# Four-head attention sum: running states stored slot by slot, and one gather at the end in place of a masked copy at every column

## The reference

```
score[e, h] = leaky_relu(a_src[src[e], h] + a_dst[dst[e], h], 0.2)
top[n, h]   = max over the edges into n, and the loop edge, of score
w[e, h]     = exp(score[e, h] - top[dst[e], h])
sum[n, h]   = sum over the edges into n of w[e, h] * x[src[e]]      (64 wide)
out[n]      = mean over h of (sum[n, h] / total weight[n, h]) @ W[h] + bias
```

## Time and profile before

| | us |
|---|---|
| median of 3 runs | 10054.14 (10051.63 to 10055.38) |
| the profiled execution, its own time | 10059.48 |
| its span, from the first to the last instruction | 10057.3 |
| DVE busy over the span | 6330.4 (63%) |
| POOL busy over the span | 6560.1 (65%) |
| PE, ACT busy | 3022.2 (30%), 2917.7 (29%) |
| copies into `head` in the four-head stage, L1328 | 175.1 in 392 |
| head sums of the four-head stage, L1325 | 341.3 in 1568 |

### The profile page before, as it was taken

The page is one execution under the profiler, slowest core; times in us unless marked ns, Lnnn a source line. Parts: engine busy times, 40 slices in busy tenths (PEclk is TensorE's granted clock), DMA queues, the critical chain, the costliest instruction groups (busy, mean ns, idle before and its releaser), DMA issues. The chain is left out here.

```text
span 10057.3 us, 92986 instructions
## 1 busy us (share of the span) xinstructions
PE 3022.2 (30%) x15231; PEld 2811.3 (28%) x15231; DVE 6330.4 (63%) x18443; ACT 2917.7 (29%) x8172; POOL 6560.1 (65%) x6186
## 2 busy tenths in 40 slices
PE   3233002111114666500666634444400002333300
PEld 2132001111114555400655534444400002333300
DVE  8999887666664767500665579999644435666600
ACT  5366234333333444300433312222200002223200
POOL 2334017777776777577777757777677777666577
PEclk7566555555556878755555555555555555665555
DMA  1010271111113544411544511111111113434311
GB/s 53 14 30 24 98 234 26 25 25 25 25 22 101 158 148 155 134 43 50 182 170 169 177 43 48 47 47 47 39 44 45 44 42 105 112 108 115 91 45 40
DMA packets 455154, 791.99 MB, mean 79 GB/s; under 512 B 119922, under 2 KB 149611, under 8 KB 454559
## 3 DMA queue, kind: packets, MB, share of 16 engines
q1 hardware_dynamic: 252126, 560.13, 16.7%
q0 software_dynamic: 188448, 201.53, 9.2%
q10 hardware_dynamic: 14112, 26.10, 0.7%
HBM read 388.06 MB, written 425.04 MB: 81 GB/s over the span
## 5 line engine op out<-in xcount | busy, mean ns | idle before, releaser
L1056 POOL DMA_INDIRECT e_other<-X,e_from_rows x392 | 610.9, 1558 | 279.5 <-DVE e_fin L1343 143.2
L1720 POOL DMA_INDIRECT e_mine<-T,e_from_rows x392 | 400.7, 1022 | 569.3 <-DVE e_from_rows L1767 450.8
L743 POOL COPY sort_spare<-sort_words 128x768 f32<-128x768 f32 x272 | 369.2, 1379 | 606.9 <-DVE sort_words L802 396.9
L3395 POOL DMA_INDIRECT e4s_mine<-XA,e4s_from_rows x392 | 407.9, 1041 | 231.9 <-DVE e4s_from_rows L3449 124.3
L2209 PE MATMUL e_turned<-ident,e_own_x 128*128 128x128 f32 x196 | 54.6, 434 | 1573.6 <-ACT e_own_x L2121 1573.6
L2357 POOL DMA_INDIRECT e_mine<-X,e_from_rows x392 | 406.6, 1037 | 183.1 <-issue 112.5
L3416 POOL DMA_INDIRECT out_rows<-e4s_out,e4s_to_rows x392 | 385.2, 983 | 191.0 <-issue 191.0
L2378 POOL DMA_INDIRECT G<-e_g_slot,e_to_rows x392 | 385.2, 983 | 180.6 <-issue 119.0
L2865 POOL DMA_INDIRECT X<-e_row,e_to_rows x392 | 424.8, 1084 | 119.5 <-issue 116.1
L1070 POOL DMA_INDIRECT X<-e_row,e_to_rows x392 | 401.8, 1025 | 140.9 <-issue 118.2
L3398 POOL DMA_INDIRECT e4s_other<-X,e4s_from_rows x392 | 402.2, 1026 | 129.4 <-issue 127.6
(11 more groups left out here) (693 smaller groups left out, 15698.4 us busy)
## 6 DMA issues: line engine op xcount, KB each, us to landing
XA<-e_n_xa SPq DMA_DIRECT2D x49, 1056.0 KB
e4s_n_xa<-XA SPq DMA_DIRECT2D x49, 1056.0 KB, 6.3
X<-e_n_row SPq DMA_DIRECT2D x49, 576.0 KB
T<-pl_row SPq DMA_DIRECT2D x98, 272.0 KB
X<-e_n_row SPq DMA_DIRECT2D x49, 528.0 KB, 3.0
X<-pl_x ACTq DMA_DIRECT2D x98, 260.0 KB, 2.7
e_n_x<-X SPq DMA_DIRECT2D x49, 520.0 KB
G<-e_n_g SPq DMA_DIRECT2D x49, 512.0 KB, 2.8
```

Of the source, the lines that this page charges most:

```text
L1056: gp.indirect_dma_start(out=other[:, h, j, :], out_offset=None, in_=others[:, :], in_offset=bass.IndirectOffsetOnAxis(ap=from_rows[:, h, 1 ...
L1720: gp.indirect_dma_start(out=mine[:, h, j, :], out_offset=None, in_=g.T0[:, :], in_offset=bass.IndirectOffsetOnAxis(ap=from_rows[:, h, 0, j ...
L3395: gp.indirect_dma_start(out=mine[:, h, j, :], out_offset=None, in_=g.XA[:, :], in_offset=bass.IndirectOffsetOnAxis(ap=from_rows[:, h, 0, j ...
```

## The change

In the stage of four heads, DVE makes no more masked copies. SP stores the states of each chunk (128 partitions x 8 x 264 floats, 1056 KB) into a new DRAM table SUMS, one row per edge slot. Behind the last chunk, POOL gathers one row of 264 floats per partition into `head`. The row's number, `head_at`, is worked out once in `lay_out_edges`: 392*p - 1 plus the number of columns that belong to the partition's first run. The stage with one head keeps its copies.

With the copies the wait between columns goes too. It is replaced by a wait for the same head's sum of the column before, ahead of each of the sums but the first four of a chunk.

```diff
         dve = [Engine(sem(f"lay_dve{s}"), "diag flags count c0 c1 c2 c3 link ready") for s in range(ORDERS)]
...
+                gp.iota(at[:, :], pattern=[[1, 1]], base=-1, channel_multiplier=T).then_inc(const, 1)
...
+                    dve[s].done(v.tensor_reduce(fix[s][:, 5:6], g.first[s][:, :], AX.X, ALU.add), "count")
...
+                    v.tensor_tensor(g.head_at[s][:, :], fix[s][:, 5:6], at_f[:, :], ALU.add)
...
+                        if c[3]:
+                            n, h = c[3].n, c[3].slot
+                            sp.wait_ge(acc.sem, acc.after(n, summed))
+                            sp.nop(nofuse=True)
+                            sp.dma_start(slot_rows(g.SUMS, n), flat(state[:, h, :, :])).then_inc(sums_kept[h], 16)
...
                 stages(gp, NCH, RING, SKEW, body)
+                if kind == "heads":
+                    for h in range(RING):
+                        gp.wait_ge(sums_kept[h], len(range(h, NCH, RING)) * 16)
+                    gp.indirect_dma_start(out=head[:, :], out_offset=None, in_=g.SUMS[:, :],
+                                          in_offset=bass.IndirectOffsetOnAxis(ap=g.head_at[s][:, :], axis=0)).then_inc(head_back, 16)
...
                     if adding:
-                        row_numbers(adding)
+                        if kind == "edge":
+                            row_numbers(adding)
                         pay_out(adding)
...
+                    if kind == "heads":
+                        v.wait_ge(sums_kept[h], k * 16)
+                        if started:
+                            need(summed, n - 1)
...
-                        if j:
+                        if j and kind == "edge":
                             need(f"head{(j - 2) % J}")
                         for q in range(H):
                             part = slice(q * D, (q + 1) * D)
+                            if j and kind == "heads":
+                                need(f"run{j - 1}_{q}")
                             run = v.scalar_tensor_tensor(out=state[:, h, j, part], in0=before[:, part], scalar=ex[:, b, 0, j, q:q + 1],
                                                          in1=pay[:, j, part], op0=ALU.mult, op1=ALU.add)
-                        acc.done(run, f"run{j}")
-                        acc.done(v.copy_predicated(head[:, :], first[:, h if j else last, j - 1:j or J].to_broadcast([P, WSTATE]), before), f"head{(j - 1) % J}")
+                            acc.done(run, f"run{j}" if kind == "edge" else f"run{j}_{q}")
+                        if kind == "edge":
+                            acc.done(v.copy_predicated(head[:, :], first[:, h if j else last, j - 1:j or J].to_broadcast([P, WSTATE]), before), f"head{(j - 1) % J}")
...
                 end_state = state[:, LAST, J - 1, :]
-                v.wait_ge(acc.sem, acc.after(NCH - 1, f"head{J - 2}"))
-                v.copy_predicated(head[:, :], first[:, LAST, J - 1:].to_broadcast([P, WSTATE]), end_state).then_inc(set_up, 1)
-                v.wait_ge(set_up, 2)
+                if kind == "heads":
+                    v.wait_ge(acc.sem, acc.after(NCH - 1, summed))
+                    v.wait_ge(head_back, 16)
+                    v.sem_inc(set_up, 1)
```

More of the change, by code:

```diff
@@ L130, in lay_out_edges @@
         scat = [sb(f"lay_scat{s}", [P, T]) for s in range(ORDERS)]
-        ends = sb("lay_ends", [1, 2])
+        ends, at, at_f = sb("lay_ends", [1, 2]), sb("lay_at", [P, 1], I32), sb("lay_at_f", [P, 1])
         fix = [sb(f"lay_fix{s}", [P, 6]) for s in range(ORDERS)]
@@ L138, in lay_out_edges @@
         loaded, spread, turned = sem.pair("lay_loaded"), sem.pair("lay_spread"), sem.pair("lay_turned")
-        dve = [Engine(sem(f"lay_dve{s}"), "diag flags c0 c1 c2 c3 link ready") for s in range(ORDERS)]
+        dve = [Engine(sem(f"lay_dve{s}"), "diag flags count c0 c1 c2 c3 link ready") for s in range(ORDERS)]
         with nc.Block() as block:
@@ L937, in attend_edges @@
         to_rows = sb("to_rows", [P, RING, J], I32)
-        first = sb("first", [P, RING, J], I32)
+        first = sb("first", [P, RING, J], I32) if kind == "edge" else None
         mine = None if kind == "edge" else sb("mine", [P, RING, J, WOWN])
@@ L978, in attend_edges @@
             "heads": "sadd score keep top fall fallen rise"}[kind]), Engine(sem(f"{name}_act"), "ex")
-        acc = Engine(sem(f"{name}_acc"), "pay weight tops " + RUN_STEPS)
+        acc = Engine(sem(f"{name}_acc"), "pay weight tops " + (RUN_STEPS if kind == "edge" else " ".join(f"run{j}_{q}" for j in range(J) for q in range(H))))
         if kind == "heads":
@@ L996, in attend_edges @@
         LAST = (NCH - 1) % RING
+        summed = f"run{J - 1}" if kind == "edge" else f"run{J - 1}_{H - 1}"
         FIX = Chunk(0, NCH, RING)
@@ L1091, in _ @@
                 v.memset(top[:, RING - 1, :, :], NEG)
-                v.memset(head[:, :], 0.0)
-                v.memset(first[:, :, :], 0)
+                if kind == "edge":
+                    v.memset(head[:, :], 0.0)
+                    v.memset(first[:, :, :], 0)
                 v.memset(state[:, RING - 1, :, :], 0.0).then_inc(set_up, 1)
@@ L1148, in loop_logs @@
                         v.wait_ge(x3_loaded[h], (c.k + 1) * 16)
-                        v.wait_ge(acc.sem, acc.after(n, f"run{J - 1}"))
+                        v.wait_ge(acc.sem, acc.after(n, summed))
                         v.wait_ge(filed[h], c.k * 16 * J)
@@ L1306, in need @@
                         v.wait_ge(acc.sem, acc.after(m, step))
-                    v.wait_ge(flagged[h], k + 1)
-                    if kind == "edge" and begun(c, RING):
-                        v.wait_ge(sums_dve.sem, sums_dve.after(n - RING, "q0"))
-                    if started:
-                        need(f"head{J - 2}", n - 1)
+                    if kind == "heads":
+                        v.wait_ge(sums_kept[h], k * 16)
+                        if started:
+                            need(summed, n - 1)
+                    else:
+                        v.wait_ge(flagged[h], k + 1)
+                        if begun(c, RING):
+                            v.wait_ge(sums_dve.sem, sums_dve.after(n - RING, "q0"))
+                        if started:
+                            need(f"head{J - 2}", n - 1)
                     for q in range(H):
@@ L1389, in _ @@
                 end_state = state[:, LAST, J - 1, :]
-                v.wait_ge(acc.sem, acc.after(NCH - 1, f"head{J - 2}"))
-                v.copy_predicated(head[:, :], first[:, LAST, J - 1:].to_broadcast([P, WSTATE]), end_state).then_inc(set_up, 1)
-                v.wait_ge(set_up, 2)
+                if kind == "heads":
+                    v.wait_ge(acc.sem, acc.after(NCH - 1, summed))
+                    v.wait_ge(head_back, 16)
+                    v.sem_inc(set_up, 1)
+                else:
+                    v.wait_ge(acc.sem, acc.after(NCH - 1, f"head{J - 2}"))
+                    v.copy_predicated(head[:, :], first[:, LAST, J - 1:].to_broadcast([P, WSTATE]), end_state).then_inc(set_up, 1)
+                    v.wait_ge(set_up, 2)
                 for q in range(H):
@@ L3858, in gnn_kernel @@
     g.XH, g.G2S, g.B2S = dram("XH", EP, 2 * D), dram("G2S", EP, D), dram("B2S", EP, D)
-    g.X2S = dram("X2S", EP, D + 8)
+    g.X2S, g.SUMS = dram("X2S", EP, D + 8), dram("SUMS", EP, HEADS * D + 2 * HEADS)
     g.XA, g.X3S, g.OUTS = dram("XA", NP, 2 * D + 4), dram("X3S", EP, D + 2), dram("OUTS", EP, D)
@@ L3884, in gnn_kernel @@
         g.index = [sb(f"index{s}", [P, 3, T + 1], I32) for s in range(ORDERS)]
-        g.first = [sb(f"first{s}", [P, T], I32) for s in range(ORDERS)]
+        g.first, g.head_at = ([sb(f"{q}{s}", [P, width], I32) for s in range(ORDERS)] for q, width in (("first", T), ("head_at", 1)))
         g.pen, g.contrib, g.same = ([sb(f"{q}{s}", [P, T]) for s in range(ORDERS)] for q in ("pen", "contrib", "same"))
```

7 lines of the change are left out of this document (5 added, 2 removed).

## The result

| kernel | us, median (range, runs) | ratio to before, 95% interval |
|---|---|---|
| before | 10052.88 (10042.53 to 10055.38, 4) | |
| after | 9946.97 (9931.33 to 9952.29, 4) | 0.9894 [0.9877, 0.9911] |

The change takes 106 us off, 1.1%; the prediction said 113 and 9941. The two profiled executions are 10059.5 and 9952.3, 107 apart. How these 107 are made up is not how the prediction made them up, and the experiments are about that.

The account below looks back on a forecast made before the run. DVE bounds the four-head stage now, POOL next. Terms -31 (first iterations), -31 (slack), -75 (POOL's need), +22 (tail) and +2 (layout) sum to -113 us, from the median 10054.1 to 9941; range 9895 to 10005, chance 0.68.

Parts of the forecast that it names:

- POOL as the next bound: Four-head stage: DVE sets the pace at 27.8 us per iteration; once it is faster, POOL's need of 25.3 binds.
- Rival A: Four-head stage: DVE stays the bound, POOL's holds shrink or it has unseen room; -157 us, 9897; chance 0.13.
- DVE alone 23.9: Four-head stage: without the copies DVE alone would need 27.8 - 3.86 = 23.9 us per iteration.
- Slack until the bound: After the first iterations: POOL falls behind, its gathers' 9.0 us of slack lasting some 8 iterations at 3.86 gained; -31 us.
- 30 iterations at POOL's need: Remaining 30 iterations of the four-head stage: POOL binds at 25.3 us each in place of 27.8; -75 us.
- rival C: Four-head stage: POOL at its worst phase, need 26.8 us, with late landings; -41 us, 10013; chance 0.12.
- The waits at the sums: DVE's sums: the new waits and register instructions cost nothing; a chunk's 32 sums take about 6.3 us, 0.195 apart.
- Rival B: DVE's sums: the waits serialise them, 0.35 us each in place of 0.195; +86 us, 10140; chance 0.05.
- The stores at nothing: SP's queue: the 49 SUMS stores of 1056 KB cost zero, with 10 us kept for the range.
- The tail, +22: End of the four-head stage: the fix waits for the head gather behind all scatters, 127 us after iteration 48, not 105.4.
- Other stages within 3 us: Stages outside the change: the forecast is wrong if they move by more than 3 us.
- The rule and the row: Rule: the skill's reason why tensor_tensor didn't stall a DMA. Row: products hold indirect gathers, mean 1558 ns against 940 undisturbed.

Follow-up runs that it names:

- e9: The changed kernel with every second scatter of a chunk left out in the four-head stage; 9864.52 us, ratio 0.9809.
- e10: The changed kernel with the three wide products on e_z replaced by reductions that read one operand; 9889.34 us, ratio 0.9832.
- e4: e2 with the sum of two wide products made by PE matmuls in place of a DVE add; 9874.28 us, ratio 0.9824.
- e3: The changed kernel without the stores of sums and without the gather of head, which stays zero; 9925.65 us, ratio 0.9877.
- e2: The changed kernel with the gather of head moved ahead of the last four chunks' scatters on POOL; 9926.09 us, ratio 0.9873.
- e11: The kernel before with only the layout's new counts and head addresses added, which nothing reads; 10048.75 us, ratio 0.9994.
- e12: The kernel before with the SUMS table and its 49 stores added, which nothing reads; 10060.89 us, ratio 1.0006.
- e6: The same program as e10, run on the second chip; 11707.81 us, ratio 1.0075 to the kernel before there.

## Why the prediction was right, and where it wasn't

*POOL as the next bound: right.* It was the step on which most hung. e9 and e10 lighten POOL in two ways and leave DVE's work: the stretch falls from 977 to 919 and 911 us. e4 lightens DVE by 84 us: 40 are won, by its holds. Rival A (DVE stays the bound) needed the waits at the scores to be absent, and they are 54 us in the stretch.

*DVE alone 23.9: right, measured 24.0 (e10) and 24.2 (e9),* as an average of three iterations of 23.3 to 23.5 and one of 26.7 to 26.9.

*First iterations, -31: measured -28.6* (190.1 against 218.7 until iteration 10).

*Slack until the bound, -31, and 30 iterations at POOL's need, -75: mis-sized.* This is the term that failed: -106 together, measured 977.4 - 1056.0 = -78.6. Two things stand in it. The need was taken as 25.3, and is 25.8 (the last 30 iterations take 774.5): 30 x 0.5 = 15. The prediction let the DMAs drift through phases with cheap meetings. The kernel settles in another pattern: each product on e_z costs about 1.0 (1.04 by e4, a third of 3.1 by e10), and e_pay with the small disturbances 2.4 (e10's POOL is busy 676.8/38 = 17.8 where 8 x 0.94 + 8 x 0.98 = 15.4): 20.2 + 3.1 + 2.4 = 25.7. This sum splits up the measured need by e10 and is no check of it. And the slack was used up from iteration 8 to 11, where the prediction had it last until 17 (by its own 25.3 the 9.0 us of slack last 9.0/1.4 = 6.4 iterations and not 8, so part of this was its own slip). In iterations 7 to 12 POOL's first gather starts 0.9, 5.2, 10.0, 13.6, 16.6 and 19.0 us after DVE's start, up to 4.8 more each time, while DVE takes 23.1 to 23.6: a need of up to 28, above even rival C's 26.8. In the timeline the gathers of chunk 8 last 11.0 in sum and the scatters that follow 12.2, 7.8 more than undisturbed. The prediction had capped this at 6.6, for four products. But in these 28.1 us DVE goes through more than one iteration of 23, and six products meet POOL's 16 DMAs: three on e_z meet gathers, the next e_pay and two more on e_z meet scatters. The six DMAs that they lengthen:

```profile
5977.90 2.31 POOL L1067 DMA_INDIRECT e_other<-X,e_from_rows  x1 [0.30 <-issue]
...
5980.51 1.87 POOL L1067 DMA_INDIRECT e_other<-X,e_from_rows  x1 [0.30 <-issue]
...
5982.69 2.00 POOL L1067 DMA_INDIRECT e_other<-X,e_from_rows  x1 [0.30 <-issue]
...
5996.55 3.10 POOL L1081 DMA_INDIRECT X<-e_row,e_to_rows  x1 [0.30 <-DVE e_fin L1368]
...
6001.25 2.20 POOL L1081 DMA_INDIRECT X<-e_row,e_to_rows  x1 [0.31 <-issue]
...
6003.75 1.90 POOL L1081 DMA_INDIRECT X<-e_row,e_to_rows  x1 [0.30 <-issue]
```

 Iterations 10 to 17 took 202.9 us where 8 x 23.9 = 191 were forecast: 12. Together 27, the difference.

*The waits at the sums: right.* Rival B is out: 32 sums in 6.35 us, no idle time ahead of any of 1568. The register instructions and waits run beside sums that are still under way.

*The stores at nothing: right.* e3 without them takes the same time as e2 with them, and the stretch of before takes 4 us more with them.

*The tail, +22: measured +24,* and for the reason given: e2, which moves the gather alone, gives back 31.9, the wait of 31.37 and half a us. That is more than the 24, since without the wait the fix would have come 99 us after iteration 48, sooner than before's 105.9: DVE's saving in the drain, which the prediction put at nothing, is hidden under this wait. Behind the fix the stage ends 4 us sooner (43.2 against 47.1), but before's second profile has 44.1 there, so nothing is read into it.

*The layout, +2: measured +1.8.*

*Other stages within 3 us: wrong.* They moved by -22, of which the experiments place 4 to 8 in the layout part and leave 13 with the programs that have the new sum code, unexplained. These -22 and the missing 27 of the steady state nearly cancel. The total that agrees within 6 us is in good part luck; for the four-head stage alone the forecast was -115, and it was -87. Two of the prediction's own signs of being wrong came: other stages moved by more than 3 us, and in two early iterations POOL's 16 DMAs took over 26.8 (27.4 and 28.1).

*The rule and the row.* The row was right: the trace's indirect gathers wait for products with two SBUF operands, and e10 shows that reductions of nearly the same length, one operand each, don't hold them. The Trainium skill, "SBUF — State Buffer", section "Who interferes with whom", says both that a tensor_tensor with two SBUF inputs contends with GpSimd's reads and that tensor_reduce never contends on this chip; both agree with e9 and e10, 1.89 to 2.29 us for gathers beside products and 0.94 to 0.96 beside reductions. Its inference that tensor_tensor did not stall a DMA because descriptor generation needs the write interface doesn't carry over to these indirect DMAs as a whole: 1.87 to 3.10 us for one of 0.94 to 0.98. They also read their row numbers from SBUF, and no run here tells which part of the DMA waits.

## What to carry to other kernels

When the bound engine gets faster, work out what the next engine needs per iteration with its stalls in the new alignment, not in the present one: here 3.9 us taken from DVE gave 2.1, and after that DVE work was worth only the 1 us per product by which it held POOL's queue. An instruction that others wait for at the end belongs ahead of whatever drains in the same queue: one gather moved forward was worth 31 us, a third of the whole change. And judge such a term by the stage, since stages that nobody touched moved by 22 us.

## What the runs showed of the hardware

- On these chips an indirect DMA on POOL that starts while a 128x2048 product of two SBUF operands runs on DVE is let go 0.8 to 0.9 us behind the product's end (3.07 us in place of 0.94); a gather beside a reduction over the same 2048 numbers, also 2.29 us, takes 0.94 to 0.96.
- The second chip ran the programs 16 to 18% longer, with gaps of 0.2 to 1.5 us between a DVE instruction and the end of the one that it waited for, and instruction times unchanged (the sums' mean 275 ns there, 273 here; products 2.29). There the program with the reductions (e6) was 0.8% slower than before, where e10 was 1.7% faster.
- Idle time at a loop's turn differs with the rest of the program: 3.4 us on DVE each fourth iteration in the four-head stage of e9 and e10 (2.1 in before: 29.5 against 27.4), and in the last stage 26.6 us in sum in before and none in after, e11 and e12.
- In e4 PE has nearly twice the matmuls in the stretch (4104 against 2282), and the mean clock granted in it is 0.73 in place of 0.54, between the levels of 1.2 GHz (0.5) and 2.4 GHz (1.0). Its busy time grew by 10% only (495 to 545 us), as a matmul of e_back took 273 ns on average over the stage in place of 413.
